# A bank of its own for the last output projections, six tiles of logits ahead of the second numerators, and other places for two top-two groups

## The reference

```python
x = x + xattn(ctx, ctx, layernorm(x), Wk, Wv, bv, Wq, bq, Wo, bo)

# linear attention, 16 heads of 64, causal over the 32 tokens of a batch
n = layernorm(x)
q, k, v = split(n @ w_qkv); gate = sigmoid(n @ w_gate)
q, k = elu(q) + 1, elu(k) + 1
numerator   = q . cumsum(k outer v)
denominator = q . cumsum(k)
x = x + (numerator / (denominator + 1e-6) * gate) @ w_out

# mixture of experts: 8 experts of 1024 hidden values, each token goes to two
n = layernorm(x)
scores = n @ gate_w.T
top_vals, top_idx = top_k(scores, 2)
weights = softmax(top_vals)
y_e = (silu(n @ w1[e].T) * (n @ w3[e].T)) @ w2[e].T
x = x + sum over the two experts of weights * y_e
```

## Time and profile before

| | us |
|---|---|
| median of 3 runs | 834.27 (832.51 to 835.47) |
| profiled execution | 833.98 |
| its span, first to last instruction | 832.1 |
| TensorE busy | 796.2 |
| VectorE busy | 637.9 |
| ScalarE busy | 564.5 |
| GpSimd busy | 281.5 |

### The profile page before, as it was taken

The page is one execution under the profiler, slowest core; times in us unless marked ns, Lnnn a source line. Parts: engine busy times, 40 slices in busy tenths (PEclk is TensorE's granted clock), DMA queues, the critical chain, the costliest instruction groups (busy, mean ns, idle before and its releaser), DMA issues.

```text
span 832.1 us, 24093 instructions
## 1 busy us (share of the span) xinstructions
PE 796.2 (96%) x9270; PEld 695.7 (84%) x9270; DVE 637.9 (77%) x1033; ACT 564.5 (68%) x879; POOL 281.5 (34%) x190
## 2 busy tenths in 40 slices
PE   6899999999999999999898999999999999999993
PEld 4566588998999999997886889888898888998883
DVE  4444543756758485676679999999999999999992
ACT  3545456554646656463147999989998999999971
POOL 0333375020220202010001545555564555555531
PEclk9999999999999999999689999999999999999997
DMA  9999920000000000005962455445555455544552
GB/s 350 416 417 414 387 79 2 2 16 16 15 28 3 28 2 28 17 15 212 423 241 69 137 147 145 134 126 140 144 147 136 126 137 146 148 136 126 135 143 37
DMA packets 31771, 115.92 MB, mean 139 GB/s; under 512 B 4465, under 2 KB 11570, under 8 KB 26578
## 3 DMA queue, kind: packets, MB, share of 16 engines
q1 hardware_dynamic: 22834, 100.17, 33.5%
q0 software_dynamic: 8864, 14.69, 8.3%
HBM read 105.27 MB, written 9.57 MB: 138 GB/s over the span
## 4 chain that ended last, share of the span: by engine, by line
PE 89%; DVE 4%; DMA 3%; issue 2%; ACT 1%; POOL 0%; POOLq 0%; SPq 0%; DVEq 0%; ACTq 0%
PE ps L536 23%; PE ps L538 22%; PE ps L537 22%; PE ps L941 4%; PE ps L757 3%; PE ps L728 2%; PE ps L589 2%; PE ps L646 2%; PE ps L601 2%; PE ps L623 1%; DMA ctx_t<-in_ctxT 1%; PE ps L904 1%; PE ps L620 1%; PE ps L829 1%; PE ps L823 1%
## 5 line engine op out<-in xcount | busy, mean ns | idle before, releaser
L1599 DVE TENSOR_TENSOR w_lo<-w,w_hi 128x1024 fp32r<-128x1024 f32 x156 | 186.5, 1217 | 0.1
L1163 ACT ACTIVATE w_hi<-w 128x1024 fp32r x156 | 161.3, 1061 | 2.8 <-DVE tile_e L1657 2.8
L522 POOL DMA_INDIRECT out_x<-y_sb,slot_row x39 | 122.5, 3142 | 119.1 <-ACT y_sb L1195 119.1
L536 PE MATMUL ps<-w_hi,xh 128*128 128x512 f32 x312 | 125.7, 403 | 0.4 <-DVE xl L1693 0.4
L538 PE MATMUL ps<-w_hi,xl 128*128 128x512 f32 x312 | 121.9, 391 | 0.0
L537 PE MATMUL ps<-w_lo,xh 128*128 128x512 f32 x312 | 121.6, 390 | 0.0
L536 PE MATMUL ps<-xT_hi,wa_hi 128*128 128x256 f32 x384 | 109.3, 285 | 1.0 <-ACT v_sb L1085 0.8
L537 PE MATMUL ps<-xT_lo,wa_hi 128*128 128x256 f32 x384 | 107.8, 281 | 0.0
L538 PE MATMUL ps<-xT_hi,wa_lo 128*128 128x256 f32 x384 | 107.8, 281 | 0.0
L1174 ACT ACTIVATE w_hi<-w_sb 128x1024 fp32r<-128x1024 f32 x78 | 82.7, 1061 | 29.9 <-DMA w_sb<-in_w 18.3
L510 POOL DMA_INDIRECT xs_sb<-xn_d,slot_row x39 | 68.1, 1746 | 95.9 <-PE ps L904 74.0
(11 more groups left out here) (219 smaller groups left out, 1761.4 us busy)
## 6 DMA issues: line engine op xcount, KB each, us to landing
w_sb<-in_w SPq DMA_DIRECT2D x78, 512.0 KB
ctx_t<-in_ctxT SPq DMA_DIRECT2D x16, 1028.0 KB, 8.8
ctx_n<-in_ctxN SPq DMA_DIRECT2D x16, 1024.0 KB
w<-in_w SPq DMA_DIRECT2D x8, 2048.0 KB, 14.3
stage<-in_w_a SPq DMA_DIRECT2D x16, 256.0 KB, 8.5
x_all<-in_x SPq DMA_DIRECT2D x4, 512.0 KB, 8.0
out_x<-x_all POOLq DMA_DIRECT2D x8, 256.0 KB, 3.1
xn_d<-xn_first POOLq DMA_DIRECT2D x6, 256.0 KB, 2.8
```

The costliest lines, as they stand in the source:

```text
L522: pool.indirect_dma_start(out, bass.IndirectOffsetOnAxis(slot_row[:, t:t + 1], 0), y_sb[:, :], None, compute_op=ALU.add).then_inc(f_st, 16)
L536: pe.matmul(dst, l_hi, r_hi, start=first, stop=False)
L1163: act.activation(w_hi[:, c, :].rearrange("p (c n) -> p c n", c=DC), w13[:, bass.ds(e, 1), c % 2, :, c // 2 * 512:(c // 2 + 1) * 512].rearr ...
L1599: dve.tensor_tensor(w_lo[:, c, :].rearrange("p (c n) -> p c n", c=DC), w13[:, bass.ds(e, 1), c % 2, :, c // 2 * 512:(c // 2 + 1) * 512].re ...
```

## The change

The projections of the last two rounds (6 and 7) go to bank 2 in place of bank 6; earlier rounds keep bank 6. The logits of tiles 0 to 5 go to bank 3, those of tiles 6 to 11 to bank 6, in place of 2 and 3; as bank 6 is also one that the numerators use, the logits from round 3 on wait for the last gated outputs (a_o). In the drain the numerators wait for the copies of the denominators (a_de), and the projection of round 7 waits for x2(6) and no longer for a_o.

On TensorE the transposes of round 3, the logits of round 2 and two matmuls on the identity now stand ahead of the second numerators, and the projection of round 7 is taken apart, with other work between its halves. On ScalarE the copies of the transposed tiles are placed to suit. On VectorE the first normalisation of the attention stands ahead of x2(6), and the first two top-two groups stand elsewhere.

```diff
--- before.py
+++ after.py
@@ -235,7 +235,11 @@
     PC = 1024
     LOW_SCALE = 2048.0
     PARTS = ((0, 6), (6, NT - 4), (NT - 4, NT))
-    LOGIT_BANK = (2, 3, 4)
+    LOGIT_BANK = (3, 6, 4)
+
+    def out_bank(r):
+        return 2 if r >= NT // 2 - 2 else 6
+
     LATE_T = NT - 4
 
     def part_of(t):
@@ -747,7 +751,9 @@
 
         def a_nums(r, s):
             wait(pe, a_norm, 2 * r + s + 1)
-            wait(pe, a_x2, r)
+            wait(pe, a_x2, r if r < NR - 1 else r - 1)
+            if r == NR - 1:
+                wait(pe, a_de, 2 * r + 2)
             wait(pe, a_vu, 4 * r + 4)
             wait(pe, a_o, 8 * r + 4 * s)
             for c in range(FC):
@@ -760,12 +766,17 @@
             m.then_inc(a_num, 1)
 
         def a_proj(r, u, s, cs=range(FC)):
-            wait(pe, a_o, 8 * r + 8)
+            if r < NR - 1:
+                wait(pe, a_o, 8 * r + 8)
+            if r == NR - 2:
+                wait(pe, a_vu, 4 * (NR - 1) + 3)
+            if r == NR - 1:
+                wait(pe, a_x2, r)
             wait(pe, a_gl, 4 * r + 2 * s + 2)
             wait(pe, a_wr, 4)
             rows = slice(s * P, (s + 1) * P)
             for c in cs:
-                m = mm3(ps[:, 6, s * D:(s + 1) * D], goh[:, c, rows], gol[:, u, c, rows], w_out_hi[:, c, :], w_out_lo[:, c, :],
+                m = mm3(ps[:, out_bank(r), s * D:(s + 1) * D], goh[:, c, rows], gol[:, u, c, rows], w_out_hi[:, c, :], w_out_lo[:, c, :],
                         c == 0, c == FC - 1)
             if s == 1 and c == FC - 1:
                 m.then_inc(a_y, 1)
@@ -816,6 +827,8 @@
 
         def g_logits(r):
             wait(pe, g_xT, r + 1)
+            if part_of(2 * r):
+                wait(pe, a_o, 8 * NR)
             bank = LOGIT_BANK[part_of(2 * r)]
             for s in range(2):
                 t = 2 * r + s
@@ -845,17 +858,20 @@
             a_nums(r, 0)
             g_trs(2)
             g_logits(1)
-            a_nums(r, 1)
             g_trs(3)
             g_logits(2)
+            wait(pe, a_x2, r)
+            for _ in range(2):
+                pe.matmul(ps[:, out_bank(r), 0:256], ident, con[:, 0:256], start=True, stop=True)
+            a_nums(r, 1)
+            g_trs(4)
             a_proj(r, u, 0)
-            a_proj(r, u, 1)
             g_logits(3)
-            g_trs(4)
             g_trs(5)
             g_logits(4)
+            a_proj(r, u, 1)
+            g_logits(5)
             g_trs(6)
-            g_logits(5)
             g_logits(6)
             g_trs(7)
             g_logits(7)
@@ -1117,14 +1133,13 @@
 
         def drain(r, u):
             den_ev(r)
-            for k in range(3):
+            for k in range(4):
                 g_xT_ev(k)
             gated_hi(r, u, 0)
+            g_xT_ev(4)
             gated_hi(r, u, 1)
-            g_xT_ev(3)
+            g_xT_ev(5)
             g_sqrt(r - 1)
-            g_xT_ev(4)
-            g_xT_ev(5)
             g_sqrt(r)
             g_xT_ev(6)
             g_xT_ev(7)
@@ -1418,7 +1433,7 @@
         def x2(r):
             rows = x_all[:, bass.ds(2 * r, 2), :].rearrange("p a d -> p (a d)")
             wait(dve, a_y, r + 1)
-            dve.tensor_tensor(rows, ps[:, 6, :], rows, ALU.add).then_inc(a_x2, 1)
+            dve.tensor_tensor(rows, ps[:, out_bank(r), :], rows, ALU.add).then_inc(a_x2, 1)
 
         def g_stats(r):
             if not valid(r, NR):
@@ -1556,22 +1571,22 @@
             g_lns(r - 2)
             recip(r, 0)
             recip(r, 1)
+            norm_att(r, 0)
             x2(r - 1)
-            norm_att(r, 0)
             recip(r, 2)
             recip(r, 3)
             norm_att(r, 1)
             gated(r, u, 0)
             gated_lo(r, u, 0)
+            top_two(0)
             gated(r, u, 1)
             gated_lo(r, u, 1)
             g_stats(r - 1)
-            top_two(0)
             g_lns(r - 1)
             x2(r)
             g_stats(r)
+            top_two(1)
             g_lns(r)
-            top_two(1)
             counts()
```

## The result

| | before | after |
|---|---|---|
| median | 835.23 us (16 runs, 832.51 to 837.59) | 838.79 us (16 runs, 836.39 to 842.51) |
| profiled execution | 833.98 | 842.51 |
| its span | 832.1 | 840.6 |

A forecast was written before the change was run, and what follows sets the result against it. TensorE, busy for 96% of the span, was taken as the bound, slowed in the drain. x2(7) 3.9 to 7.5 us late, then 2.2 us gained to 1.3 lost up to the ranks: +1.7 to +8.8, middle +5, 839.0 us; range 832.0 to 842.5.

The forecast's parts named there:

- the tail: Stretch from x2(7) to the rank matmuls: 13.2 us before, 11.0 to 14.5 after, so 2.2 us gained to 1.3 lost.
- The stop for issue: TensorE stops at late 256-instruction blocks: the numerators' stop goes, one comes behind the projection's 9th row, 6.7 us a block.
- Ahead of the second numerators: Transposes, logits and two filler matmuls fill TensorE's 1.41 us wait; the fillers themselves cost up to 1.77 us.
- The clock: In the last projection it returns at 412.8 us, giving x2(7) at 418.2, or through the second half, giving 421.9.
- the sum's early case: Clock back at 412.8 us, end of the projection's first half; the rest takes 5.5 us and x2(7) starts at 418.2.
- Where the projection ends: x2(7) now also waits for logits and transposes between the projection's halves: 1.06 + 0.52 + 1.06 us at high clock.
- The last normalisation behind the group: On VectorE the second top-two group goes ahead of the last normalisation and holds it up by 2.44 us.
- No new stop: Rival: no or only a short stop in the last projection; +0.1 to +3.6 us, middle +1.8, 835.8 us; chance 0.28.
- The clock doesn't fall: Rival: TensorE's clock stays high into the projection and the block comes quickly; 2.2 us faster, 830 us; chance 0.15.
- The weight transfers as the new bound: Rival: later weight loads would bound the kernel after the drain; given no chance.
- The signs: Drain signs if right: 1 to 4 us pause behind projection row 9, mostly 0.21 us rows, x2(7) at 418 to 422.
- The row prices: Cost of a row of the last projection on TensorE: 0.21 us at low clock, 0.12 us at high.

The follow-up runs named there:

- the shifted kernel before: The kernel before with 64 more semaphore waits at TensorE's start, moving its instructions by 32 against the 256-instruction blocks; 843.82 us, ratio 1.0121, median spoiled by a late start.
- kernel 4: The changed kernel with the two halves of the last projection next to each other again; 835.76 us, ratio 1.0017 to the kernel before.
- kernel 1: The changed kernel with the second top-two group back behind the last normalisation; 837.35 us, ratio 1.0034 to the kernel before.
- kernel 7: The changed kernel without the two added filler matmuls ahead of the second numerators; 837.03 us, ratio 1.0026 to the kernel before.
- 8: The changed kernel with projection halves together, second group behind the normalisation, no added fillers, and three instead of six filler matmuls ahead of the ranks; 834.64 us, ratio 0.9993.
- 11: The changed kernel with projection halves together, second group behind the normalisation and no added fillers, six fillers ahead of the ranks kept; 835.46 us, ratio 0.9997.
- 9: The changed kernel once more, unedited, for a second profile; 843.87 us in one run, drain 41.8 us.
- 12: The kernel before with three instead of six filler matmuls ahead of the ranks; 836.58 us, ratio 0.9998 to the kernel before.
- kernel 2: The changed kernel with 320 more semaphore waits at TensorE's start, moving its instructions by 160 against the blocks; 852.27 us, ratio 1.0217, median spoiled by a late start.
- kernel 6: The changed kernel with the expert weight transfers issued only after the last logits; 864.46 us in one run, only its drain of 34.8 us counts.
- the mended kernels: Two versions of the changed kernel with projection split, second group's move and added fillers undone, with three or six fillers ahead of the ranks; 834.64 and 835.46 us.

## Why the prediction was right, and where its sizes were off

The forecast was +5 us within +1.7 to +8.8. The runs give 3.2 to 5.5 us, and the two profiles of the drain +4.2 and +7.3 us. That the total came so near the middle is partly luck. In the first profile x2(7) is 2.6 us late, where the forecast's parts had 3.9 to 7.5, and the tail is 1.6 us longer, where they had 2.2 shorter to 1.3 longer: one part was too high and the other too low. By its steps:

- **The stop for issue.** Right in its place and its cause. The count of 256 instructions gave the rows at which TensorE stopped in the changed kernel (14 and 9), in the kernel without fillers (18 and 13) and in the shifted kernel before (16 and 3). That the block is late because of the full DMA engines was argued; the drains without transfers show it. The size was off on both sides: the block in the projection takes 5.0 us (kernel 4), 5.1 (1), 5.9 (7, 8 and 11), and 6.2 (the changed kernel, twice), not 6.7, which is what the numerators' block took in the kernel before, twice; but the stop took 2.43 us and not 1.6, because the ninth row came early, at the high clock.
- **Ahead of the second numerators.** The cost of up to 1.77 us for the fillers, which the sum took in full, was mis-sized. Up to the numerators they cost nothing, since the block of the numerators arrives 8.7 to 9.5 us into the drain whatever precedes it (kernels 7, 8, 9, 11, 12 and both of before), and at the numerators' end they cost 0.5 us (kernel 7). Against that, the time filled there gains nothing either: TensorE was bound by the block, not by the gated outputs.
- **The clock.** I had it come back at the end of the first half or through the second. It came back with the first row of the projection, 12.0 us into the drain, fell again in the stop and rose again with the end of the first half, at 18.5. The first of these rises bought nothing: the nine rows that it made faster only lengthened the stop, which ends with the block. From the block to x2(7) it took 420.36 - 411.94 = 8.4 us, and the sum's early case has 418.2 - 409.6 = 8.6. That x2(7) is 2.6 us late and not 3.9 comes mostly from the block: it arrived 15.8 us into the drain, where the sum has 409.6 - 392.84 = 16.8. Half of that 1.0 us is an earlier start, since the clock fell behind the logits of round 1 and not within them, and half is a block of 6.2 us in place of 6.7. In the second profile x2(7) is 6.2 us late, by the case in which the clock stays low through the projection.
- **Where the projection ends.** Right. The pieces between the halves took 2.1 us, where the sum has 1.06 + 0.52 + 1.06 = 2.6 at the high clock. Kernel 4 undoes the split and has x2(7) 4.4 us earlier than this profile, 2.4 earlier than kernel 1.
- **The last normalisation behind the group.** I had 2.44 us on VectorE; it is 2.1, and the ranks see 0.6 to 1.1 of it (tails of 14.0 and 14.5 us against 13.4 in kernel 1). The tail was to be 2.2 us shorter to 1.3 longer; it is 1.6 and 1.0 longer, at the late end. TensorE idles 1.59 us for the normalisation, and the clock is low from there to the ranks.
- **The rivals.** "No new stop" did not happen; kernels 2 and 6 show what it would have been, a drain of 33.4 to 34.8 us, so 1.1 us shorter to 0.3 longer than before, where the rival had +1.8. "The clock doesn't fall" did not happen in either profile; in the second it was still high up to the first row of the projection, 10.5 us into the drain, which was nearly its condition, and that drain was the longer one: the block stopped TensorE all the same. The weight transfers as the new bound did not happen.
- **The signs.** The pause behind the ninth row of the projection and the second group ahead of the normalisation came in both profiles. Matmul rows of 0.21 us in the larger part of the projection did not come in the first: 13 of its 48 rows were at the low clock. They came in the second, where all were. Counted from the drain's start, x2(7) was to lie between 25.2 and 29.2 us; it lay at 24.2 and 27.8.
- **The row prices.** The sum divides by 22 and 29 rows; the timeline has 21 rows between 406.33 and 410.95 and 27 from there to 414.34. Row starts are 0.21 and 0.12 us apart even so, so the sum stands.

The term furthest off is thus the fillers' 1.77 us, which measured 0.5 us at the numerators' end. What stays open is the share of each part in the medians, since three parts undone one by one give 1.5 + 2.9 + 2.2 = 6.6 us and together 4.6, with uncertainties of about 2 us each. Also open is why the mended kernels' drains, 1.4 and 2.6 us shorter than before in their profiles, show so little in the medians: one profile each doesn't give the mean of a drain, and the end of the program alone differs by more than 1 us between profiles, by the clock in the last tile.

## What to carry to other kernels

Before moving work into a wait, ask what ends that wait once the named one is gone: here it was the arrival of the next block of instructions, slowed by the weight transfers, and the work moved ahead bought nothing that the medians show. Count instructions from a stop for issue to find the next places where one can stand. Don't put work that the next step doesn't need ahead of the last producer of a chain: the logits ahead of the second half of the projection, 2.1 us, and the group ahead of the last normalisation, 0.6 to 1.1 us in the tail, made a good part of the loss; the stop in the projection, with the clock behind it, came on top.

## What the runs showed of the hardware that I had not expected

- Behind late blocks of instructions more was lost than their stops. The same program up to x2(7) took 22.2, 24.2 and 27.8 us there in three executions, with stops of 1.7, 2.4 and 3.3 us in all; the clock was low for 7, 10 and 17 us of it. That the longer stops took the clock down is likely but not shown apart.
- A block took 5.0 to 6.7 us with the DMA engines at a share of 1.0, and at most 3.1 us with a share of 0.09 (one reading, kernel 6). The Trainium skill ("Runtime: NRT & Kernel Launch", Instruction fetch mechanics) has the cost of crossing a block "mostly hidden"; in these drains it was hidden with idle DMA engines, and with full ones it showed as 1.6 to 3.6 us of stops, kernel 2 alone excepted.
- 320 waits on a semaphore that had already been reached moved the first matmul from 7.12 to 24.57 us, which is 55 ns for each; 64 of them moved it from 7.02 to 10.07, which is 48 ns each.
